# Cross-attention of a decoder layer on one core: one mask product per sequence, and a head average by adding transposes

## The reference, cut to what matters

```
Q = (x_text @ Wq).reshape(Bb, Tt, H, DH)                     # H = 4 heads of 32
K = (x_vision @ Wk).reshape(Bb, Gg, H, DH)
scores = einsum('bthd,bghd->bhtg', Q, K) / sqrt(DH)
scores = where(vision_mask[:, None, None, :], scores, -inf)
topv, topi = top_k(scores, 32)
probs = softmax(topv)
attn = zeros_like(scores).at[bi, hi, ti, topi].set(probs)
attn_mean = attn.mean(axis=1)                                # over the heads
c_t = einsum('btg,bgd->btd', attn_mean, x_vision @ Wv) * text_mask[..., None]
```

## Time and profile before

| | |
|---|---|
| median of three runs | 7286.86 us (7278.25 to 7288.03) |
| profiled execution | 7288.94 us, its span 7287.1 us |
| busy in the span | PE 6717.7, DVE 5404.4, ACT 4452.2, POOL 4596.0 us |
| mean granted clock of PE | 0.955 |
| the first pass's scans | from 215 to 5056 us |

### The profile page before, as it was taken

How to read it: one execution, slowest core, us unless ns; L and a number is a source line. 1 busy time by engine, 2 the same in 40 slices (tenths; PEclk the granted TensorE clock), 3 DMA queues, 4 the chain that set the end, 5 groups by cost and what they waited for, 6 DMA issues and landing times. The chain is left out here.

```text
span 7287.1 us, 107870 instructions
## 1 busy us (share of the span) xinstructions
PE 6717.7 (92%) x25168; PEld 3749.4 (51%) x25168; DVE 5404.4 (74%) x13962; ACT 4452.2 (61%) x9788; POOL 4596.0 (63%) x3991
## 2 busy tenths in 40 slices
PE   3899999999999999999999999997789999999997
PEld 1354455554555444454445554554656666666664
DVE  5588888888888888888888888886336666666665
ACT  2788888788887888878888788885212212221111
POOL 0788888888888888888888888897011111111111
PEclk6999999999999999999999999998789999999998
DMA  1556556665566656656556565555611111111110
GB/s 41 137 146 150 137 143 157 148 151 142 143 154 154 145 142 142 148 153 149 143 137 152 157 149 145 139 154 170 204 36 35 32 32 32 32 32 32 32 32 20
DMA packets 554213, 835.19 MB, mean 115 GB/s; under 512 B 169179, under 2 KB 207388, under 8 KB 551712
## 3 DMA queue, kind: packets, MB, share of 16 engines
q1 hardware_dynamic: 552768, 820.23, 44.5%
q10 hardware_dynamic: 864, 8.65, 0.3%
HBM read 745.91 MB, written 74.45 MB: 113 GB/s over the span
## 5 line engine op out<-in xcount | busy, mean ns | idle before, releaser
L1255 POOL TENSOR_TENSOR arena<-arena 128x512 f32<-128x512 f32 x2048 | 2588.2, 1279 | 308.3 <-DVE arena L1180 258.6
L877 PE MATMUL psum<-arena 128*128 128x512 f32 x4096 | 2156.2, 622 | 30.0 <-POOL arena L1255 24.0
L1180 DVE TENSOR_TENSOR_SCAN arena<-arena,psum 128x512 f32<-128x512 f32 x1024 | 1236.4, 1207 | 379.5 <-ACT arena L1049 292.6
L1268 POOL TENSOR_TENSOR arena<-arena 128x512 f32<-128x512 f32 x1024 | 1334.5, 1303 | 121.8 <-PE psum L877 121.4
L1036 ACT ACTIVATE arena<-arena 128x128 f32<-128x128 f32 x4096 | 1301.8, 394 | 141.6 <-PE psum L862 141.0
L1184 DVE TENSOR_TENSOR_SCAN arena<-psum,arena 128x512 f32<-128x512 f32 x1024 | 1234.4, 1205 | 86.7 <-issue 38.7
L877 PEld LDWEIGHTS psum<-arena 128*128 128x128 f32 x4096 | 703.9, 197 | 570.0 <-issue 379.4
L1834 POOL TENSOR_SCALAR arena<-arena 128x4 f32<-128x4 f32 x160 | 36.8, 230 | 1164.9 <-DVE arena L1695 1164.9
L1049 ACT ACTIVATE arena<-arena 128x508 f32<-128x508 f32 x1024 | 735.9, 719 | 57.9 <-DVE arena L1180 57.1
L862 PEld LDWEIGHTS psum<-arena 128*128 128x128 f32 x4096 | 515.5, 146 | 492.9 <-issue 438.5
L1049 ACT ACTIVATE psum<-arena 128x508 f32<-128x508 f32 x1024 | 699.7, 683 | 50.5 <-DVE arena L1180 31.0
(11 more groups left out here) (218 smaller groups left out, 10304.8 us busy)
## 6 DMA issues: line engine op xcount, KB each, us to landing
arena<-bc_scratch SPq DMA_DIRECT2D x1152, 512.0 KB, 5.2
arena<-in_xT_dram SPq DMA_DIRECT2D x32, 512.0 KB
arena<-in_x_dram SPq DMA_DIRECT2D x32, 512.0 KB, 7.7
x_scratch<-arena SPq DMA_DIRECT2D x32, 512.0 KB, 5.6
xin_scratch<-arena SPq DMA_DIRECT2D x128, 128.0 KB, 2.5
arena<-kernel_scratch SPq DMA_DIRECT2D x32, 512.0 KB, 6.4
arena<-x_scratch SPq DMA_DIRECT2D x32, 512.0 KB, 3.7
out_dram<-arena SPq DMA_DIRECT2D x32, 512.0 KB
```

The source lines that it names most:

```text
L877: pe.matmul(y_ps, ident, ring[:, u % RING], start=False, stop=n == NS - 1).then_inc(S["nsum"], 1)
L1180: dve.tensor_tensor_scan(s, decay_sb[:, u // 2 % 2], bx_ps[:, u // 2 % 2], 0.0, ALU.mult, ALU.add)\
L1255: pool.tensor_tensor(h, h, Cb[:, u // 2 % PAIRS, u % 2], ALU.mult).then_inc(S["hc"], 1)
L1268: pool.tensor_tensor(ring[:, u % RING], uu[par][:, c], Bb[:, state(u)], ALU.mult)\
```

## The change

- `sc{b}`: one mask product per sequence, of one row of `ones` by the mask row repeated four times (512 columns), opens the whole bank; the four score products add to it, each with its wait as before.
- `dg{b}`: ScalarE no longer scales the identity into `diag`; it scales the four probability tiles `sc[:, h]` in place. It waits for `em` (VectorE's masking) in place of the average before.
- `at{b}`: the four products by `diag` become four products by the identity in the transposing form (`is_transpose=True`), which add up in the same PSUM region. The wait for `em` goes.
- The tile `diag` (512 columns of SBUF) is no longer carved out, so the tiles after it move.

```diff
--- before.py
+++ after.py
@@ -81,7 +81,7 @@
     decay=64, bx=32, bxt=32, bxp=32, scan=64, hc=64, nsum=64, y=4, yg=4,
     o_mm=2, res=2, st1=4, mv1=1, ve1=1, rs1=1, nm1=1, nb1=1, x1=4, st2=4, mv2=1, ve2=1, rs2=1, tmb=1,
     xt_mm=2, x1T=2, q_mm=1, k_mm=1, qT=1, kT=1, maskb=1, s_mm=16,
-    v8=4 * KR, took=4 * KR, nmax=4, ex=4, em=4, rinv=4, rq=4, diag=4, at_mm=4, atT=4,
+    v8=4 * KR, took=4 * KR, nmax=4, ex=4, em=4, rinv=4, rq=4, scaled=4, at_mm=4, atT=4,
     xa_mm=2, xaT0=1, xaT1=1, film_mm=4, film_mul=4, film=4,
 )
 
@@ -540,7 +540,6 @@
         qT, kT = cv.f32(T), cv.f32(T)
         sc = cv.f32(H * P).rearrange("p (h g) -> p h g", h=H)
         left = cv.f32(H * P).rearrange("p (h g) -> p h g", h=H)
-        diag = cv.f32(H * P).rearrange("p (h g) -> p h g", h=H)
         at = cv.f32(T).rearrange("p (b t) -> p b t", b=G)
         xa0, xa1 = cv.f32(T), cv.f32(T, CT2 + 1)
         stats = cv.f32(G * 6).rearrange("p (b s) -> p b s", b=G)
@@ -815,22 +814,21 @@
                         need(pe, "maskb", i, 1)
                     else:
                         need(pe, "em", i, b)
+                    pe.matmul(ps, ones[0:1], maskb[0:1, b * L:(b + 1) * L][:, None, :].to_broadcast([1, H, L]),
+                              start=True, stop=False)
                     for h in range(H):
                         rows = slice(h * HD, (h + 1) * HD)
                         if h:
 
                             need(pe, "s_mm", i, b * H + h)
-                        o, row = ps[:, h * P:(h + 1) * P], slice(h * HD, h * HD + 1)
-                        pe.matmul(o, ones[row], maskb[row, b * L:(b + 1) * L], start=True, stop=False)
-                        pe.matmul(o, qT[rows, b * L:(b + 1) * L], kT[rows, b * L:(b + 1) * L],
-                                  start=False, stop=True).then_inc(S["s_mm"], 1)
+                        pe.matmul(ps[:, h * P:(h + 1) * P], qT[rows, b * L:(b + 1) * L], kT[rows, b * L:(b + 1) * L],
+                                  start=False, stop=h == H - 1).then_inc(S["s_mm"], 1)
                 elif name[:2] == "at":
                     b = int(name[-1])
                     ps = bank(f"a{b}")
-                    need(pe, "em", i, b + 1)
-                    need(pe, "diag", i, b + 1)
+                    need(pe, "scaled", i, b + 1)
                     for h in range(H):
-                        mm = pe.matmul(ps[:, 0:L], sc[:, h], diag[:, h], start=h == 0, stop=h == H - 1)
+                        mm = pe.matmul(ps[:, 0:L], sc[:, h], ident, start=h == 0, stop=h == H - 1, is_transpose=True)
                     mm.then_inc(S["at_mm"], 1)
                 elif name == "xa":
                     for n, (lo, hi) in enumerate(((0, P), (P, CTX))):
@@ -1000,13 +998,10 @@
                     need(act, "tmb", i, 1)
                     act.activation(rq, rinv, ACT.Identity, scale=tmb[:, c:c + 1]).then_inc(S["rq"], 1)
                     need(act, "rq", i, c + 1)
-                    if c:
-                        need(act, "at_mm", i, c)
-                    else:
-                        need(act, "at_mm", i - 1, G)
+                    need(act, "em", i, c + 1)
                     for h in range(H):
-                        a = act.activation(diag[:, h], ident, ACT.Identity, scale=rq[:, h:h + 1])
-                    a.then_inc(S["diag"], 1)
+                        a = act.activation(sc[:, h], sc[:, h], ACT.Identity, scale=rq[:, h:h + 1])
+                    a.then_inc(S["scaled"], 1)
                 elif name[:2] == "at":
                     need(act, "at_mm", i, c + 1)
                     if c == 0:
```

## The result

The changed kernel takes 7275.35 us (median of 20 runs, 7245.04 to 7293.71), the kernel before 7288.02 (20 runs beside them, 7273.06 to 7300.96): ratio 0.998, 95% interval 0.9973 to 0.9988. The difference of the medians is 12.7 us where 13.4 were forecast. In a second comparison the medians were 7274.31 and 7280.43, the ratio 0.9987 (0.9973 to 1.0). The profiled execution took 7281.31 us, its span is 7279.5, its mean granted clock 0.947 against 0.955 before. The total came out as said, but two of its terms did not, and they cancel.

A forecast was written before the change was run, and what follows sets the result against it. No single engine bounds the first pass; the bound moves within each block, TensorE setting 71 us. Terms -12.9 + 0 + 0 - 0.5 = -13.4 us from 7286.86 give 7273.5, stated as 7274; range 7242 to 7302.

The forecast's parts named there:

- `at0` to `at2` at 0: First three head averages of a block: making them transposes gains 0, as waits or other full engines cover it.
- the 34 us stretch: Part of a block after TensorE's full 71 us: VectorE busy 30.65, ScalarE 31.66, TensorE said to reach its end before them.
- `at3` at 0.43 us a block: Fourth head average, before the next block's in-projection: transposes save 0.43 us in 30 of 32 blocks, 12.9 us.
- from it to the scores of the next block TensorE never waits: From the fourth head average to the next block's scores: no TensorE wait, so its 0.43 us arrive in full.
- The scores at 0, -7 to +14: Wide mask product at `sc0`, end of TensorE's full stretch: taken as 0, bounds -7 to +14 us over 31 blocks.
- my own price of 3.2 us for a 0.66 window: After the x-projection: a block whose ten-us window has granted clock 0.66 takes 38.8 us to VectorE's L1111, otherwise 35.6.
- the clock falls more often: Between `sc0` and `sc1` and behind `at1`: 3.2 us slower per further block with a 0.66 window, priced 7304; chance 0.15.
- late windows changing from 11 by more than four: Test of the forecast: wrong if stretches with clock below 1.00 after the x-projection change from 11 by over four.
- The rule on transposes: Skill page's claim that the full clock does not engage for transposes; forecast said it fails where they stand among products.
- the 71 us stretch: From one block's head average to the next block's scores: TensorE busy 70.91 of 71.00, granted clock 1.00, transposes included.
- A pair of blocks takes 0.9 us less: Expected sign in the trace after: two blocks together 0.9 us shorter than a pair with the same clock before.
- Wrong if blocks shorten by more than 1 us each: Test of the forecast over the blocks: it fails if each becomes more than 1 us shorter.

The follow-up runs named there:

- wide mask alone: Kernel before with only the score part changed, one wide mask product per sequence, averages still products with scaled identities: 7307.28 us, ratio 1.0017.
- averages alone: Changed kernel without its score part, adding transposes for all four averages but four narrow mask products per sequence: 7258.36 us, ratio 0.9942; again 7247.92, 0.9958.

## Why the prediction was right, and where only its sum was

**`at0` to `at2` at 0: right.** Shown by the kernel in which these three alone transpose, which equals wide mask alone (both 1.0017); a block without a fall takes 150.11 us in the one and 150.12 in the other. One of the readings behind it was wrong all the same: in the 34 us stretch TensorE is busy 32.03 us, more than VectorE and ScalarE, so that row does not show that it had reached its end before them.

**`at3` at 0.43 us a block: right in kind, too small.** The row is 0.47 against 0.96, so 0.49 at the place itself, and a block without a fall is 0.4 us shorter: 150.05 us before (x-projections 2082.54 and 2232.59), 149.64 with the averages alone (1770.72 and 1920.36). But the step "from it to the scores of the next block TensorE never waits" was read in one block whose start is not at the loop's jump. At every second block start the jump lies in between. With `at3` transposing, the standstill there is shorter and the clock stays up. In five blocks that is 3.2 us each: 16 us on top of 12.9 makes 29, and the two kernels that split `at3` from the other three lie 30 apart. The traces bear it out: the first pass is 28.9 us shorter with the averages alone than before, with the same late falls. How 0.4 us earlier becomes 0.6 us less of standstill in the mean is not settled by the runs; for nine of the 13 jumps the profile names no releaser (issue).

**The scores at 0, -7 to +14: the length right, the price wrong.** `sc0` is 0.04 us longer, x 31 = 1 us, and a block without a fall takes 149.75 us against 149.67 with narrow masks. The term that was mis-sized is the clock's. By my own price of 3.2 us for a 0.66 window, eight more of them are +26; four 0.83 ones fewer, at half the price, -6; one fall more at a block start, +3. The first passes of the two traces lie 29 us apart (4557.0 and 4527.9), which leaves 4 to 6 for the four early falls, 1 to 2 us each. In medians the kernel after lies 26 us above the averages alone in the second comparison (7274.31 - 7247.92), by the ratios 28 in the first and 21 in the second.

**The rival "the clock falls more often": true, as a part.** Its place was named rightly (between `sc0` and `sc1`, and behind `sc1`), its price too. What I held against it, that the columns of the products stay the same and only `sc1`'s are issued otherwise, was the mistake: the fall follows what TensorE does inside the score step, and the wide product changes just that. How it does so is not shown: the narrow masks too stand behind the waits from head to head and not in them, and half-wide ones, at every second head, make fewer falls than narrow ones. I gave it 0.15 as an alternative to the forecast; it came beside it. The criterion that I had set, late windows changing from 11 by more than four, was not met (15 and 12) and missed the point: the sum of late windows hardly moves while 0.83 ones turn into 0.66 ones and a new place opens.

**The rule on transposes.** The averages alone has every average as a transpose and its late falls are 11 and 8, no more than 11 before, none early. So it is not the transposes that bring the clock down here. By the Trainium skill's TensorE: Matmul & The Clock Gate, Part 4: PE-mode transpose, the full clock does not engage for transposes. The traces do not agree with that for transposes among products: in the 71 us stretch of the kernel after the granted clock is 1.00.

**"A pair of blocks takes 0.9 us less".** With no fall in it, a block takes 0.3 us less in the kernel after (149.75 against 150.05) and 0.4 with the averages alone, so a pair 0.6 and 0.8. **"Wrong if blocks shorten by more than 1 us each":** in the change they don't. With the averages alone the medians give 36 / 30 = 1.2 us, which is these 0.4 and the block start.

So -13.4 forecast and -12.7 measured is a hit of the sum by two errors that cancel, and that is luck: a gain of some 29 us at `at3` instead of 12.9, and a cost of 21 to 28 us of the wide mask product instead of 0. So is the nearness of the two numbers, for the second comparison has -6.1. The averages alone gained 36 and 33 us in the medians of the two comparisons, 28.9 and 34.3 in the first passes of their traces. The prices give 27 and 34 there: 11 for the blocks, 16 for the five falls at the jump, and in the second trace 6 for one 0.66 and two 0.83 windows fewer. The version to take is the change with two half-wide mask products for the wide one: 0.994 of before in the same comparison in which the change itself has 0.9987.

What stays open: how the wide product brings the falls about, why two products of half width make fewer falls than four narrow ones, and one or two wide ones more. The records in a score step (nine with the wide one, ten with it twice, ten with the half-wide ones, twelve with narrow ones) don't order them. Nor was the kernel before with half-wide masks and product averages run.

## What to carry to other kernels

Before replacing several small products by one wide one, look at the waits between them, though they are short: TensorE's granted clock follows how it is fed, and a step that is hardly longer (2.16 us against 2.12 here) can cost 3.2 us behind it. Count clock windows over all blocks of both traces, by place and by value, before explaining a small difference in time, and look in which part of the span the difference lies. And run the parts of a change singly even when the sum fits: here one half was worth three times the whole.

## What the runs showed that I had not expected

- Whether a block falls differs between blocks that issue the same instructions at the same distances (1.00 in the window at 1785.77 of the kernel after, 0.66 in the one at 2393.91, four blocks on). The Trainium skill's TensorE: Matmul & The Clock Gate, Part 1, calls the window of the clock's monitor free-running, so that where the clock changes depends on where in it the work lands; the counts of two executions of one kernel (14 and 10 of 0.66) agree with that, though no run here moved the start by itself.
- A fall behind a score step begins while every record says that TensorE is busy (3.40 of 3.40 us at 0.53): filling the waits of the 2 us ahead, which the view calls 92% busy, took it away.
- fp32 transposes that add into one PSUM region cost as much as plain ones: 0.44 us for four, half of the same four as products.
- A bf16 product of one row and 512 columns delays the next product by 0.22 us, less than the 0.28 that I had taken for its lower bound.
